# A decoder block on one core: q turned to head-inner order by ScalarE, and a rearranged start and passage

## What is computed

```python
q = _split_qk(x @ Wq.T, b, n) * SCALE          # 2*H = 32 half heads of D = 16
k = _split_qk(x @ Wk.T, b, n)
v = (x @ Wv.T).reshape(b, n, H, 2 * D).transpose(0, 2, 1, 3)
att = jnp.einsum('bnqd,bnkd->bnqk', q, k)      # heads against heads, token by token
att = jax.nn.softmax(att.astype(jnp.float32), axis=-1)
diff = att[:, :, :H, :H] - lam * att[:, :, H:, H:]
out = jnp.einsum('bnah,bhnd->bnad', diff, v)
out = out * jax.lax.rsqrt(jnp.mean(out * out, axis=-1, keepdims=True) + EPS)
out = out * (1.0 - LAM_INIT)
return out.reshape(b, n, DIM) @ Wo.T + bo
# then
x = _layernorm(x + attention(x))
x = _layernorm(x + x * scan(r -> decay * r + ctx * ctx))
x = _layernorm(x + mlp(x))                     # ternary weights, relu squared, rms norm
```

## Time and profile before

| | |
|---|---|
| median of 3 runs | 1162.05 us (1158.12 to 1164.16) |
| the profiled execution | 1160.84 us, of which the span is 1159.0 us |
| mean granted TensorE clock | 0.956 of 2.4 GHz |
| PE busy | 1042.1 us (90%), 6992 matmul records |
| DVE busy | 926.5 us (80%) |
| ACT busy | 565.7 us (49%) |
| POOL busy | 243.5 us (21%) |
| first phase | to about 451 us |
| passage | about 451 to 557 us |
| second phase | 557 us to the end |

### The profile page before, as it was taken

How to read it: one execution, slowest core, us unless ns; L and a number is a source line. 1 busy time by engine, 2 the same in 40 slices (tenths; PEclk the granted TensorE clock), 3 DMA queues, 4 the chain that set the end, 5 groups by cost and what they waited for, 6 DMA issues and landing times.

```text
span 1159.0 us, 20344 instructions
## 1 busy us (share of the span) xinstructions
PE 1042.1 (90%) x6992; PEld 825.5 (71%) x7008; DVE 926.5 (80%) x1668; ACT 565.7 (49%) x866; POOL 243.5 (21%) x237
## 2 busy tenths in 40 slices
PE   6799999899998998443799999999999999999994
PEld 5577676676776776333688888888888888888883
DVE  4368888888888999968678797997979969789555
ACT  5323333343433342310656666575665675656672
POOL 5211252525252525050602002020020010200000
PEclk9899999999999999666799999999999999999997
DMA  7967696859596868786321311412114113100010
GB/s 279 279 159 174 141 239 142 238 140 241 140 244 143 205 148 203 199 239 227 122 42 37 74 37 36 109 36 67 42 36 109 36 34 74 37 34 4 1 37 36
DMA packets 165671, 139.71 MB, mean 121 GB/s; under 512 B 139872, under 2 KB 139872, under 8 KB 159456
## 3 DMA queue, kind: packets, MB, share of 16 engines
q1 hardware_dynamic: 94432, 113.57, 35.8%
q10 hardware_dynamic: 71168, 25.17, 8.6%
HBM read 82.09 MB, written 52.43 MB: 116 GB/s over the span
## 4 chain that ended last, share of the span: by engine, by line
PE 64%; DVE 20%; ACT 5%; issue 4%; DMA 3%; SPq 2%; POOL 1%; ACTq 1%; DVEq 0%; POOLq 0%
PE ps_f L670 20%; PE ps_s L686 19%; PE ps_f L533 9%; PE ps_o L621 7%; PE ps_s L550 5%; DVE row_sum L1012 2%; DVE sc L995 1%; DVE row_max L998 1%; DVE st L989 1%; SPq L389 1%; DVE o_sb L1045 1%; PE ps_f L621 1%; DVE st L1023 1%; DVE sc L993 1%; DVE xtl L961 1%
## 5 line engine op out<-in xcount | busy, mean ns | idle before, releaser
L670 PE MATMUL ps_f<-x2h,w 128*128 128x512 f32 x512 | 204.8, 400 | 1.6 <-DVE x2l L1193 1.6
L670 PE MATMUL ps_f<-x2l,w 128*128 128x512 f32 x512 | 201.4, 393 | 0.0
L686 PE MATMUL ps_s<-w,hh 128*128 128x512 f32 x500 | 196.6, 393 | 0.0
L686 PE MATMUL ps_s<-w,hl 128*128 128x512 f32 x500 | 194.9, 390 | 0.0
L533 PE MATMUL ps_f<-xth,wh 128*128 128x512 f32 x384 | 159.4, 415 | 12.9 <-DVE xtl L961 9.6
L1201 DVE TENSOR_TENSOR hl<-h_sb,hh 128x512 fp32r<-128x512 f32 x128 | 95.5, 746 | 94.5 <-ACT hh L885 94.4
L533 PE MATMUL ps_f<-xtl,wh 128*128 128x512 f32 x384 | 150.6, 392 | 0.0
L533 PE MATMUL ps_f<-xth,wl 128*128 128x512 f32 x384 | 150.6, 392 | 0.0
L550 PE MATMUL ps_s<-qbd,k 128*32 128x128 f32 x2048 | 125.1, 411 | 17.7 <-DMA qbd<-q_scr 17.4
L1391 POOL TENSOR_TENSOR xb<-xb,bob 128x512 f32<-128x512 f32 x32 | 47.4, 1512 | 430.5 <-DMA xb<-in_x 430.5
L550 PEld LDWEIGHTS ps_s<-qbd,k 128*32 128x32 f32 x2048 | 83.4, 147 | 54.1 <-DMA qbd<-q_scr 15.4
(11 more groups left out here) (134 smaller groups left out, 1807.1 us busy)
## 6 DMA issues: line engine op xcount, KB each, us to landing
x_raw<-in_x_turned SPq DMA_DIRECT2D x8, 1024.0 KB, 7.5
q_scr<-f_sb ACTq DMA_DIRECT2D x32, 256.0 KB, 3.8
k_scr<-f_sb ACTq DMA_DIRECT2D x32, 256.0 KB, 2.6
w_scr<-w_in SPq DMA_DIRECT2D x16, 512.0 KB, 5.2
v_scr<-f_sb ACTq DMA_DIRECT2D x32, 256.0 KB, 5.6
k<-k_scr SPq DMA_DIRECT2D x8, 1024.0 KB, 8.0
qbd<-q_scr SPq DMA_DIRECT2D x128, 64.0 KB, 4.2
v<-v_scr SPq DMA_DIRECT2D x64, 128.0 KB, 5.6
```

Of the source, the lines that this page charges most:

```text
L670: last = nc.tensor.matmul(ps_f[:, j % 2, :], w1[:, j // 2, k, (j % 2) * P:(j % 2 + 1) * P], xx[:, k, :], start=(k == 0 and xx is x2h), sto ...
L686: last = nc.tensor.matmul(ps_s[:, t, :], a[:, j % 4, t * P:(t + 1) * P], w2[:, j, :], start=(j == 0 and a is hh), stop=(j == HC - 1 and a ...
```

## The change

1. **q.** `q_scr` is laid out by lane, so that a chunk of q is written in 256-byte pieces as k and v are. SP reads one half of the block's q in one DMA into a new staging buffer `q_stage` (`q_load`), which shares its memory with that half of `xth` that is not being projected. ACT turns it to head-inner order in two instructions for each half (`q_turn`), and SP copies it lane by lane into `qbd` in eight DMAs (`qbd_load`). `qbd` is now ordered (group half, lane, group, head). The scores read `qbd[:, c % 2, :, group, :]`, 16 heads side by side.
2. **x columns.** The columns of x are given in another order (`lanes_apart`), so group numbers and the eviction of v change; v is read back in one DMA instead of eight.
3. **Start.** The q weights and x of block 0 come in four quarters each, in turn, and PE multiplies the first two chunks quarter by quarter (`project_first`). Wo's halves are written after the first q and k have been requested, and have their own place in memory.
4. **Order in the first phase.** Scores calls 2 and 3 stand at chunks 5 and 7 (before 6 and 8), the third exponential before the ninth eviction, the x copies at n = 9 (before 7), the last group sums at 11 (before 10); `o_write` moves by one body. Bodies 2 and 3 are written out, and the loop runs once.
5. **Passage.** `out_lower(0)` and the out projections of block 0 come before the end of the last softmax; the four projections use four PSUM banks; `scan` comes before `x1_norm`; `dbd_load(7)` comes before `o_write(6)`; the turning, squaring and scaling of block 7's output (`mixed_turn`, `mixed`, `square_sum`, `o_scale`) move into the first body of the second phase, where the bias comes first on POOL.

```diff
 def lane_slot(t):
-    return (t % 4) * 2 + t // 4
+    return (t // 2 % 2) * 4 + t // 4 * 2 + t % 2
...
-        qbd = sb("y", "qbd", [P, LANES, H, G], F32)
+        qbd = sb("y", "qbd", [P, 2, LANES, G // 2, H], F32)
...
-        AT_SCORES = (0, 1, 6, 8)
+        AT_SCORES = (0, 1, 5, 7)
...
-        AT_SUMS = (4, 5, 10, 10)
+        AT_SUMS = (4, 5, 11, 11)
...
         def proj_bank(i, t):
-            return ps_o[:] if later(i) else ps_f[:, t % 2, :]
+            return ps_o[:] if later(i) else (ps_f[:, 0, :], ps_f[:, 1, :], ps_t[:], ps_o[:])[t]
...
-            def q_load(i, s):
+            def q_load(i, s, place):
+                sp.dma_start(q_in(place), q_scr[i, s].rearrange("t (d a) g -> (t d) a g", a=H)).then_inc(qin_ld, 16)
+
+            def qbd_load(place):
                 for t in range(LANES):
-                    sp.dma_start(qbd[H * t:H * (t + 1), lane_slot(t), :, :],
-                                 q_scr[i, s * 256:(s + 1) * 256, t * G:(t + 1) * G]
-                                 .rearrange("(d a) g -> d a g", a=H)).then_inc(qbd_ld, 16)
+                    sp.dma_start(qbd[H * t:H * (t + 1), :, lane_slot(t), :, :],
+                                 q_turned(place)[H * t:H * (t + 1)]).then_inc(qbd_ld, 16)
...
-            def first_half_load(i):
-
-                hold(*([(s_ps, at(i, 16, 0))] if later(i) else [(zeroed, 2), (wo_wr, 32)]),
-                     *f_written(i, (0, 1, 5, 6, 7)))
-                k2_load(i)
-                q_load(i, 0)
-
-            def second_half_load(i):
-                hold((s_ps, at(i, 16, 8)), *f_written(i, (2, 3)))
-                q_load(i, 1)
+            def first_half_in(i, place):
+
+                hold(*([(q_tn, at(i, 4, 0))] if later(i) else []), *f_written(i, (0, 1)))
+                q_load(i, 0, place)
+
+            def first_half_load(i, place):
+
+                hold(*([(s_ps, at(i, 16, 0))] if later(i) else [(zeroed, 2), (wtr_lo, 12)]), (q_tn, at(i, 4, 2)))
+                qbd_load(place)
+
+            def second_half_in(i, place):
+
+                hold((f_ps, at(i, 12, 12)), *f_written(i, (2, 3)))
+                q_load(i, 1, place)
+
+            def second_half_load(i, place):
+                hold((q_tn, at(i, 4, 4)), (s_ps, at(i, 16, 8)))
+                qbd_load(place)
...
-            qkvo_load(0)
-            sp.dma_start(x_raw[:, 0, :, :], xt_in[0]).then_inc(xa_ld, 16)
+            for k in range(KC):
+                sp.dma_start(w_raw[:, 0, k, :], w_qkvo[0, :, k, :]).then_inc((*wq_part, wraw_ld[0])[k], 16)
+                sp.dma_start(x_raw[:, 0, k, :], xt_in[0, :, k, :]).then_inc((*x_part, xa_ld)[k], 16)
...
+            w1_load(0)
+            hold((ot_hi, 1), (ot_lo, 1), (cx_sq, TT))
+            load_first(1)
+            dbd_load(NSB - 1)
+            w1_load(1)
             o_write(NSB - 2)
-            dbd_load(NSB - 1)
...
                     last = nc.tensor.matmul(ps_s[32 * j:32 * (j + 1), 2 * (c % 2) + gq // 4,
                                                  (gq % 4) * P:(gq % 4 + 1) * P],
-                                            k2[:, :, g], qbd[:, :, :, g].rearrange("p a b -> p (a b)"),
+                                            k2[:, :, g], qbd[:, c % 2, :, j * 8 + gq, :],
                                             start=True, stop=True)
...
             def x_upper(i, par, k):
-                if k == 0:
+                if k == 0 and later(i):
+                    act.wait_ge(qbd_ld, at(i - 1, 256, 128))
...
+            def q_turn(i, c, place):
+                gh = c % 2
+                if gh == 0:
+                    act.wait_ge(qin_ld, at(i, 32, 16 * (c // 2 + 1)))
+                    if c or later(i):
+                        act.wait_ge(qbd_ld, at(i, 256, 128 * (c // 2)))
+                nc.scalar.activation(q_turned(place)[:, gh, :, :].rearrange("p (j g) a -> p j g a", j=4),
+                                     q_in(place).rearrange("p a (h g j) -> p h j g a", j=4, h=2)[:, gh, :, :, :],
+                                     ACT.Copy).then_inc(q_tn, 1)
...
+                    if do_1 and n == 1:
+                        q_turn(i - 1, 2, 1 - par)
+                        q_turn(i - 1, 3, 1 - par)
+                    if n == 5:
+                        q_turn(i, 0, 1 - par)
+                        q_turn(i, 1, 1 - par)
...
             mixed_turn(NSB - 2, 3)
+            out_lower(0)
+            square_sum(NSB - 2, 2)
             soft_second(NSB - 1, 2)
-            square_sum(NSB - 2, 2)
+            soft_first(NSB - 1, 3)
             square_sum(NSB - 2, 3)
             rms_seed(NSB - 2)
-            soft_first(NSB - 1, 3)
             soft_second(NSB - 1, 3)
             diff_turn(NSB - 1)
-            out_lower(0)
             for t in range(TT):
                 add_projection(0, t)
```

More of the change, by code:

```diff
@@ L200, in program @@
         xa_ld = sem("xa_ld")
+        wq_part = [sem(f"wq_part{k}") for k in range(KC - 1)]
+        x_part = [sem(f"x_part{k}") for k in range(KC - 1)]
         xt_hi, xt_lo = sem("xt_hi"), sem("xt_lo")
@@ L310, in phase_a @@
             body(1, 1, False, True)
-            with eng.Fori(1, NSB // 2 - 1) as h:
+            body(2, 0, True, True)
+            body(3, 1, True, True)
+            with eng.Fori(2, NSB // 2 - 1) as h:
                 body(h * 2, 0, True, True)
@@ L529, in project @@
                         pe.wait_ge(wtr_lo, n + k + 1)
-                    if n == 0 and not later(i):
-                        pe.wait_ge(xt_lo, k + 1)
                     for w, xx in ((wh, xth), (wh, xtl), (wl, xth)):
@@ L588, in w_sums, with project_first @@
                 nc.tensor.matmul(sums_bank(u, r), blk[:], w_b[:, half(r)], start=True, stop=True).then_inc(wt_ps, 1)
+            def project_first():
+                for k in range(KC):
+                    pe.wait_ge(wtr_lo, k + 1)
+                    pe.wait_ge(xt_lo, k + 1)
+                    for n in range(2):
+                        for w, xx in ((wh, xth), (wh, xtl), (wl, xth)):
+                            last = nc.tensor.matmul(ps_f[:, n, :], w[:, 0, k, n * P:(n + 1) * P], xx[:, 0, k, :],
+                                                    start=(k == 0 and xx is xth and w is wh),
+                                                    stop=(k == KC - 1 and w is wl))
+                        if k == KC - 1:
+                            last.then_inc(f_ps, 1)
             def body(i, par, do_2, do_1):
                 for n in range(12):
-                    project(i, n, par)
+                    if later(i) or n >= 2:
+                        project(i, n, par)
+                    elif n == 0:
+                        project_first()
                     if do_2 and n in AT_MIX:
@@ L775, in _ @@
                 w_upper(0, k)
-            for k in range(KC):
                 x_upper(0, 0, k)
@@ L857, in ctx_square @@
                     act.wait_ge(cx_ld, at(i, 16, 16))
+                    if not later(i):
+                        act.wait_ge(qbd_ld, 256 * NSB)
                     if later(i):
@@ L930, in body_b @@
                             ctx_square(i + 1, AT_CTX.index(j))
-                    if j == 6:
+                    if not later(i) and j < 4:
+                        mixed(NSB - 1, j)
+                    if j == (6 if later(i) else 9):
                         act.wait_ge(x2_done, at(i, TT, TT))
@@ L1017, in soft_second @@
                 kept = sc[:, c % 2, :, s * H:(s + 1) * H]
+                if c == 0 and not later(i):
+                    v.wait_ge(wo_wr, 32)
                 if s == 0:
@@ L1396, in _ @@
             o_scale(NSB - 2)
-            o_scale(NSB - 1)
             def body_b(i, prep, fin, ahead):
@@ L1402, in body_b @@
                         add_bias(i + 1, t)
+                if not later(i):
+                    o_scale(NSB - 1)
             phase_b(pool, body_b)
```

152 lines of the change are left out of this document (90 added, 62 removed).

## The result

The changed kernel takes **1176.7 us** (median of 4 runs, 1175.3 to 1179.1), the kernel before 1163.1 beside it (4 runs, 1158.1 to 1166.4): ratio 1.012, 95% interval 1.008 to 1.016, slower by 14 us. The prediction, 1121.5 us with a range of 1104 to 1146, is wrong in size and in sign.

The account below looks back on a forecast made before the run. The prediction took VectorE to bound the first phase and TensorE the second. Gains of 9.7 + 6.1 + 7 + 13.5 + 3 = 39.3 us off 1160.84 gave 1121.5 us, range 1104 to 1146.

Parts of the forecast that it names:

- What bounds the first phase: First phase: it runs at VectorE's pace, 345.7 us for six bodies; most of TensorE's gaps are waits for VectorE.
- The faster scores: Scores calls: 3.92 to 2.2 us each, 54 us of TensorE time over 32 calls, mostly not path time.
- Rival (d): Scores calls: the turned layout brings TensorE nothing, calls stay at 3.9 us; 1131.5 us in all, chance 0.04.
- The middle bodies: Five middle bodies of the first phase: 1.4 us gained in each, 7 in all (2 to 11).
- rival (c): Six first-phase bodies: ScalarE's turns wait for late staged q, delaying VectorE's squares; slower than before, e.g. 1170 us; chance 0.05.
- The slower clock: Middle bodies: TensorE, idle some 5 us a body, may run its next projections at 1.2 GHz instead of 2.4.
- Start: Start to VectorE's first scores transposition: 60.66 comes down to 51, 9.7 us gained (6 to 13).
- First body: Body following the first scores: two VectorE waits for TensorE go, exponential's wait falls to 1.27; 6.1 us gained (4 to 7).
- rival (b): Whole kernel: new waits eat the middle bodies and half the rest; 1149 us (1142 to 1155), chance 0.12.
- Passage: Last first-phase body to first MLP matmul: otl and projections move under the fourth softmax; 13.5 us gained (8 to 17).
- the 0.8 charged for it: Passage: last block's dbd lands late, mixing ends at 522 to 526 where VectorE wants it at 522.5; 0.8 us lost.
- First MLP body: First body of the second phase: bias wait of 3.7 us goes, 0.7 charged for moved work; 3 gained (-1 to 5).

Follow-up runs that it names:

- e5: Changed kernel with k evicted from PSUM in another order, so keys of four successive scores matmuls lie 64 bytes apart and are still right: 1154.5 us, ratio 0.993.
- e2: Changed kernel with the keys of four successive scores matmuls 64 bytes apart, pairing queries with wrong keys: 1154.5 us, ratio 0.992.
- e7: e5 with SyncE, in the very first body, copying the turned q into qbd before the weight write and next weight load: 1154.4 us.

## Why the prediction was wrong, point by point

**What bounds the first phase**: right as far as it went. DVE sets the pace; in the changed kernel's six bodies it still starts each one without a wait for scores. But I counted only waits between the engines. That what PE reads could make DVE's own instructions longer was in no term. The faster calls by themselves do not (e5, at 1.93 to 1.98 us a call); the neighbouring keys do.

**The faster scores**: right, 3.92 to 2.2 us a call (1.93 to 1.98 in e5). Rival (d) is out.

**The middle bodies** is the step that failed. My list held waits and the price of the turns, and nothing for a changed index: the diff takes the key of matmul (gq, j) at 4m + j instead of 16j + m, and I gave that "x columns in another order" no term, because it adds no instruction. It costs 22 us (e5 against the changed kernel), 20.5 of them in the six bodies. Without it those bodies are at 347.4 us where I forecast about 339, and the five middle ones take 58.35 us each, as before. In four bodies of e2, which behave as e5's, DVE waits 7.4 us for squares and 4.5 for exponentials,

```profile
DVE o_ms L1137 <- ACT o_sq L882: 7.4, 8, 1.2
DVE row_sum L1097 <- ACT sc L876: 4.5, 4, 1.1
DVE o_sb L1132 <- PE ps_o L612: 3.5, 6, 1.0
```

against 8.9, 7.8 and 1.5 before. The exponential's wait fell to 1.1 a body, as forecast. The wait for squares, of which I had 1.3 a body going, fell by 0.4 (in e5 by 0.1); it did not grow behind the turns either, so rival (c) is out. The wait for the mixing grew by 0.5 (in e5 by 0.2), and DVE itself is busy 1.0 us more a body, half of it because the scaling by lam (L1110) now always lies beside GpSimd (1.33 instead of 1.05 us). A gain of 1.4 a body was sized on waits of 0.7 to 2.0 us, and shifts of that size elsewhere cancel it.

The slower clock that the prediction feared is there. A middle body of e5, windows (columns as in the earlier trace rows) and PE's row that ends the gap:

```profile
236.00:239.00 3.00, 0.00 (x0) 0.00 (x0) 2.90 (x4) 3.00 (x4) 0.00 (x0) 0.50 0.55 175
239.00:242.60 3.60, 3.55 (x8) 2.81 (x9) 3.53 (x5) 2.63 (x4) 0.00 (x0) 0.50 0.71 135
```

```profile
239.05 0.80 PE L575 MATMUL ps_f<-xth,wh 128*128 128x512 f32 x1 [3.73 <-ACT f_sb L851]
```

PE has waited 3.31 us for dbd and then 3.73 for an eviction that stands behind an exponential and two turns on ScalarE. The granted clock is 0.50 (1.2 GHz) there, once in every middle body for 6.8 to 10.2 us, where the kernel before has 1.00 in all its middle bodies. The mixing result for which DVE then waits 0.56 comes behind the slow matmuls. No run separates this from the rest.

**Start**: +3.5, or +4.7 in e5, of 9.7. The turns were done on time:

```profile
30.98 2.20 ACT L870 ACTIVATE q_stage<-q_stage 128x512 f32<-128x512 f32 x2
...
46.58 2.19 ACT L836 ACTIVATE xth<-x_raw 128x512 fp32r<-128x512 f32 x4 [5.45 <-DMA qbd<-q_stage]
```

I had 32.7 for their end, and it was 33.2. Then I let SP issue at once. But the weight write and the next weight load stand ahead of the copies, each with its hold:

```profile
35.23 0.34 SPq L441 DMA_DIRECT2D w_scr<-w_in  x1
38.00 0.33 SPq L433 DMA_DIRECT2D w_in<-in_proj_turned  x1
38.44 5.81 SPq L383 DMA_DIRECT2D qbd<-q_stage  x8
```

Those holds were missed, and e7 shows a second chain, the next weights, that ends at the same time. Whether both together are worth the other 5 us is not shown.

**First body**: +6.1 forecast, -2.7 in e5, and -5.2 with the slowing on top. PE's two late scores calls are gone, as said. What I had not counted is a stretch of full DMA queues: from 45 to 62.6 us the DMA engines are 1.00 busy at 338 GB/s (before 0.97 at 273, in a stretch in which the first scores were still waited for). ScalarE's timeline in the changed kernel:

```profile
62.59 0.60 ACT L851 ACTIVATE f_sb<-ps_f 128x512 f32<-128x512 f32 x1 [6.07 <-DMA v_scr<-f_sb]
...
79.12 2.08 ACT L870 ACTIVATE q_stage<-q_stage 128x512 f32<-128x512 f32 x2 [3.94 <-DMA q_stage<-q_scr]
```

Transfers of the Wo halves, x, the staged q and the last v are all issued between 45 and 53. ScalarE waits 6.07 us for an old v write, so the turns behind it and SP's copies are late, and PE waits for them with the third call:

```profile
77.01 2.76 PE L592 MATMUL ps_s<-qbd,k 128*32 128x128 f32 x64 [2.46 <-DMA qbd<-q_stage]
```

DVE waits 3.36 us for the group sums that PE runs after this call. Then ScalarE waits 3.94 for q, and DVE waits 3.25 for x behind those turns. This is rival (b)'s kind of price, in a place where I had put none. I did not test by a run which of those writes it hangs on.

**Passage**: right, +14.8 for 13.5, and by the path forecast. DVE's waits in it fall from 15.2 us to 3.3, and its work by 2.7. The wait of 25.83 us for otl is down to 8.4; dbd is the later one, as the prediction said. But the 0.8 charged for it were not lost: the mixing that it holds ends at 544.63, PE transposes the scan right behind it, and DVE, busy all the time, takes the result up at 547.75. PE's waits in the passage, then all that DVE waits there:

```profile
PE ps_o L612 <- DMA dbd<-dt: 15.9, 1, 15.9
PE ps_s L612 <- DMA dbd<-dt: 11.5, 1, 11.5
PE ps_f L680 <- DVE otl L1215: 8.4, 1, 8.4
```

```profile
DVE x2l L1280 <- ACT x2h L952: 3.3, 4, 1.9
```

**First MLP body**: +3 forecast, -6.0. DVE's wait of 3.7 us for the bias is gone, but PE gains nothing by it: it waits 3.7 us for DVE's addition, as before, since DVE is now busy with the transpositions and square sums moved in. A further 3.3 us comes through the late output of that block. The argument that the second product runs three steps behind was no cover, since its banks in PSUM are those that the moved mixing results occupy (PE L744 waits 1.2 us for o_sb).

**The whole**: the changed index accounts for 22 of the 55 us between forecast and measurement. e5, without it, takes 1154.5 us, still 33 over the forecast and outside its range: start 5, first body 9, middle bodies 9 and first MLP body 9 to 10 short. So each gain outside the passage was counted too high by itself, by waits of engines behind the one that I had followed.

Of the rivals none named the mechanism. Only (c) had the direction, by a wait; the loss came from longer instructions. (b), new waits everywhere, with 1142 to 1155, fits e5's time, but not its stages: the passage, which (b) had at 8, gave 15.2, and the first body and the first MLP body lost. The 2 us that the prediction puts on every DMA under (c) stand in the section of the Trainium skill that it names (DMA: Bandwidth & Descriptors, anatomy of one DMA) for DMAs that GpSimd issues. Here SyncE issues them, and the shortest median landings of the changed kernel are 2.3 us (`dbd`, 64 KB) and 2.7 (`qbd`, 64 KB).

## What to carry to other kernels

When several small matmuls run side by side in different quarters of the array, look at where each one's operands lie: keep the stationary operands of concurrent ones at least 16 bytes apart per partition, and the moving ones too (of these only 4 bytes, which conflict, and 64, which do not, were run). A diff that only permutes an index adds no instruction and still wants a term. After any change compare busy time at equal instruction counts first: if it grew, look for what lies beside the longer ones, before looking for waits.
